# Attention scores in whole chunks with wider masks, pairs of heads in straight code, projections in four pieces

## The reference

```
scores = jnp.einsum('bhqd,bhkd->bhqk', qh, k_rec) / math.sqrt(d)
t = jnp.arange(s, dtype=jnp.float32)
decay = jnp.exp(-LAMBDA_DECAY * jnp.abs(t[:, None] - t[None, :]))
scores = scores * decay[None, None, :, :]
attn = jax.nn.softmax(scores, axis=-1)
out = jnp.einsum('bhqk,bhkd->bhqd', attn, v_rec)
```

## Time and profile before

| | |
|---|---|
| median of three runs | 1450.16 us (1449.71 to 1453.62) |
| the profiled execution | 1457.08 us, span 1453.1 us |
| busy in the span: TensorE, ScalarE, VectorE, GpSimd | 1307.9, 1059.6, 711.9, 624.5 us |
| mean granted TensorE clock | 0.956 |
| score matmuls, product matmuls | 2432, 4096 |
| exponentials of a half | 1024, busy 866.0 us |
| masks, far reads | 512 and 248 |

### The profile page before, as it was taken

How to read it: one execution, slowest core, us unless ns; L and a number is a source line. 1 busy time by engine, 2 the same in 40 slices (tenths; PEclk the granted TensorE clock), 3 DMA queues, 4 the chain that set the end, 5 groups by cost and what they waited for, 6 DMA issues and landing times. The chain is left out here.

```text
span 1453.1 us, 27412 instructions
## 1 busy us (share of the span) xinstructions
PE 1307.9 (90%) x8496; PEld 582.6 (40%) x8497; DVE 711.9 (49%) x1948; ACT 1059.6 (73%) x1419; POOL 624.5 (43%) x745
## 2 busy tenths in 40 slices
PE   7879999999999999999999999999987867889881
PEld 4623333333333333333333333333335546657541
DVE  5525535454453535445354443333324566685754
ACT  4558898987989888898988899999953534544532
POOL 2525444443445444444444444444202543333574
PEclk9979999999999999999999999999988987999996
DMA  7775566654566655556665566546962224457843
GB/s 195 252 179 132 136 153 159 128 146 109 134 152 147 158 119 145 124 124 160 143 161 103 145 126 134 105 97 135 244 127 73 91 91 153 160 189 225 248 126 106
DMA packets 141170, 212.00 MB, mean 146 GB/s; under 512 B 56864, under 2 KB 102816, under 8 KB 132768
## 3 DMA queue, kind: packets, MB, share of 16 engines
q1 hardware_dynamic: 134496, 192.86, 53.6%
q0 software_dynamic: 6144, 16.79, 3.6%
q10 hardware_dynamic: 384, 0.52, 0.1%
HBM read 147.19 MB, written 67.11 MB: 147 GB/s over the span
## 5 line engine op out<-in xcount | busy, mean ns | idle before, releaser
L841 ACT ACTIVATE work<-ps 128x1024 f32<-128x1024 f32 (+1 forms) x1024 | 866.0, 928 | 139.4 <-DVE ps L638 109.2
L764 PE MATMUL ps<-work 128*32 128x512 f32 x4096 | 551.4, 611 | 4.3 <-POOL work L607 3.6
L752 PE MATMUL ps<-Q_st,K_st 64*128 64x512 f32 (+3 forms) x2432 | 422.8, 423 | 33.6 <-ACT work L841 14.3
L604 POOL TENSOR_TENSOR work<-work 128x512 f32<-128x512 f32 x248 | 257.9, 1040 | 413.5 <-DVE work L646 413.5
L752 PEld LDWEIGHTS ps<-Q_st,K_st 64*128 64x128 f32 x2432 | 225.0, 185 | 515.8 <-ACT work L841 259.9
L646 DVE TENSOR_SCALAR work<-ps 128x512 f32<-128x512 f32 x248 | 171.2, 690 | 286.5 <-PE ps L752 286.1
L638 DVE TENSOR_TENSOR ps<-ps,small 128x128 f32<-128x128 f32 x512 | 150.6, 298 | 261.7 <-PE ps L752 254.9
L607 POOL TENSOR_SCALAR work<-work 128x512 f32<-128x512 f32 x248 | 154.3, 622 | 49.1 <-POOL work L604 49.1
L764 PEld LDWEIGHTS ps<-work 128*32 128x32 f32 x4096 | 82.1, 108 | 128.5 <-issue 73.5
L2219 POOL DMA_INDIRECT xT<-y_dram,decay x64 | 65.5, 1023 | 62.8 <-DMA xT<-y_dram,decay 27.7
L2201 POOL DMA_INDIRECT xs_dram<-part,decay x64 | 66.5, 1039 | 56.2 <-DMA xs_dram<-part,decay 24.7
(11 more groups left out here) (184 smaller groups left out, 1149.9 us busy)
## 6 DMA issues: line engine op xcount, KB each, us to landing
K_st<-halves_dram SPq DMA_DIRECT2D x248, 256.0 KB, 5.5
halves_dram<-work SPq DMA_DIRECT2D x64, 512.0 KB, 3.9
Q_st<-halves_dram SPq DMA_DIRECT2D x248, 128.0 KB, 5.8
work<-xs_dram SPq DMA_DIRECT2D x96, 128.0 KB, 2.6
y_dram<-work SPq DMA_DIRECT2D x48, 256.0 KB, 2.8
work<-in_L_attn_x SPq DMA_DIRECT2D x16, 512.0 KB, 7.3
attn_dram<-work SPq DMA_DIRECT2D x16, 256.0 KB, 6.9
work<-attn_dram SPq DMA_DIRECT2D x8, 512.0 KB, 4.5
```

The costliest lines, as they stand in the source:

```text
L604: nc.gpsimd.tensor_tensor(p, p, p, ALU.mult).then_inc(s_["far_sq"], 1)
L752: m = nc.tensor.matmul(ps[:, half_of(turn, s, k) + c % 2, q0 % CH:q0 % CH + w], K_st[tile, par, a, kt * P:(kt + 1) * P], Q_st[tile, par, a ...
L764: m = nc.tensor.matmul(ps[STRIP * c:STRIP * (c + 1), ACC + par], Vg[:, par, kt], probs[:, probs_of(turn, s), chunk(c)], start=s == 0, stop ...
L841: nc.scalar.activation(probs[:, probs_of(turn, s), chunks[0] * CH:(chunks[-1] + 1) * CH], src, ACT.Exp, scale=SCALE).then_inc(s_["exp_done ...
```

## The change

- A chunk of scores is always one matmul. `decay_of` chooses the factors for the whole chunk: for the own chunk FALL if the tile lies in its first half, RISE if in its second. `score_pieces` and `cut` go.
- With it the mask has to mend all that lies on the wrong side of the own block within the chunk: 128, 256, 256 or 128 columns for the four places of a tile in its chunk (`own_chunk`). It reads a window of one table of 512 columns, `wide_mask`, which is loaded in the prologue by one DMA of 256 KB instead of two of 64 KB.
- The own half is the second one in every tile (`OWN = 1`).
- On TensorE the order of a step is now: scores of both halves, then the products of step s-2.
- A projection's two products are issued separately: at steps 6 and 7 for the first, 11 and 12 for the second, behind the products of the step. VectorE's three pieces for the second move from steps 12, 13, 14 to 13, 14, 15.
- All 16 pairs are written out, without a loop.
- GpSimd no longer increments a semaphore of its own between the square and what follows.

```diff
 def pairs(eng, pair):
-    pair(0, True, True, False, 0)
-    with eng.Fori(1, 1 + 3 * RING, RING) as it:
-        for j in range(RING):
-            pair(it + j, True, False, False, (1 + j) % RING)
-    for it in range(1 + 3 * RING, NPAIR - 1):
-        pair(it, it < NPAIR - PPU, False, False, it % RING)
-    pair(NPAIR - 1, False, False, True, (NPAIR - 1) % RING)
+    for it in range(NPAIR):
+        pair(it, it < NPAIR - PPU, it == 0, it == NPAIR - 1, it % RING)
...
+    def decay_of(kt, c):
+        if c == kt // CT:
+            return FALL if kt % CT < CT // 2 else RISE
+        return FALL if c > kt // CT else RISE
...
+    OWN = 1
     def half_at(kt, k):
-        return k if first_half(kt) == 0 else 1 - k
+        own = kt * P // HALF
+        return own if k == OWN else 1 - own
...
+    def own_chunk(turn, s, kt):
+        bank, at = half_of(turn, s, OWN) + kt // CT % 2, kt % CT
+        if at < CT // 2:
+            width = (at + 1) * P
+            return ps[:, bank, 0:width], wide[:, CH // 2 - width:CH // 2]
+        return ps[:, bank, at * P:CH], wide[:, CH // 2:CH // 2 + (CT - at) * P]
...
 (GpSimd, far_probs)
-                pool.sem_inc(far_link, 1)
...
 (VectorE)
-                wait(dve, "sc_ps", n * NHALF + 2 * s + own_at(kt) + 1)
-                nc.vector.tensor_tensor(own_block(turn, s, kt), own_block(turn, s, kt), dmask, ALU.mult).then_inc(s_["masked"], 1)
+                wait(dve, "sc_ps", n * NHALF + 2 * s + OWN + 1)
+                own, mended = own_chunk(turn, s, kt)
+                nc.vector.tensor_tensor(own, own, mended, ALU.mult).then_inc(s_["masked"], 1)
...
-                        if prep and par == 0 and s >= 12 and s < 15:
-                            prepare(s - 12, it % PPU, 1, 2 * it + 1, idle)
+                        if prep and par == 0 and s >= 13:
+                            prepare(s - 13, it % PPU, 1, 2 * it + 1, idle)
...
 (TensorE)
-                for q0, w, a in score_pieces(kt, half):
-                    c = q0 // CH
+                for c in (2 * half, 2 * half + 1):
+                    a = decay_of(kt, c)
                     tile = slice(c % 2 * TILE_ROWS, (c % 2 + 1) * TILE_ROWS)
...
+                    m = nc.tensor.matmul(ps[:, half_of(turn, s, k) + c % 2], K_st[tile, par, a, kt * P:(kt + 1) * P],
+                                         Q_st[tile, par, a, half * CH:(half + 1) * CH], start=True, stop=True)
...
-                        scores(first, turn, n, s, 0, order, not end)
+                        for k in range(2):
+                            scores(first, turn, n, s, k, order, not end)
                         if s >= 2:
                             products(turn, n, s - 2, order, not end)
...
-                        scores(first, turn, n, s, 1, order, not end)
...
-                            if s == 7:
+                            if s == 6:
                                 wait(pe, "w", it + 1)
                                 if not first:
                                     wait(pe, "att_sb", n)
-                                project(at, 0, idle)
+                                project(at, 0, 0, idle)
+                            if s == 7:
+                                project(at, 0, 1, idle)
                             if s == 11:
                                 wait(pe, "proj_free", 2 * it + 1)
-                                project(at, 1, idle)
+                                project(at, 1, 0, idle)
+                            if s == 12:
+                                project(at, 1, 1, idle)
```

More of the change, by code:

```diff
@@ L237, in _ @@
                     sp.dma_start(decay[STRIP * r:STRIP * (r + 1), sign, :], io["c_decay"][sign]).then_inc(dec_in, 16)
-            for mask, dst in enumerate(diagonal_masks(small)):
-                sp.dma_start(dst, io["c_diag"][mask]).then_inc(dec_in, 16)
+            sp.dma_start(wide_mask(small), io["c_wide"]).then_inc(dec_in, 16)
             for n in range(4, NB):
@@ L439, in attention @@
     part = carve(work, 13312, 2, 2, 2, CH)
-    dmask, _ = diagonal_masks(small)
+    wide = wide_mask(small)
     rden = carve(small, 256, CT, QC)
@@ L722, in _, with project @@
             prime(pe, *"proj_ps sc_ps pv_done oT_ps".split())
-            def project(at, which, bank):
-                for k in range(KD):
-                    m = nc.tensor.matmul(ps[:, bank], w_unit[:, which, k], xT[:, k, at:at + CH] if isinstance(at, int) else xT[:, k, bass.ds(at, CH)],
-                                         start=k == 0, stop=k == KD - 1)
-                m.then_inc(s_["proj_ps"], 1)
+            def project(at, which, k, bank):
+                m = nc.tensor.matmul(ps[:, bank], w_unit[:, which, k], xT[:, k, at:at + CH], start=k == 0, stop=k == KD - 1, skip_group_check=True)
+                if k == KD - 1:
+                    m.then_inc(s_["proj_ps"], 1)
             def far_read(first, n, s, k, order):
@@ L747, in scores @@
                     far_read(first, n, s, k, order)
-                for q0, w, a in score_pieces(kt, half):
-                    c = q0 // CH
+                for c in (2 * half, 2 * half + 1):
+                    a = decay_of(kt, c)
                     tile = slice(c % 2 * TILE_ROWS, (c % 2 + 1) * TILE_ROWS)
-                    at = c // 2 * CH + q0 % CH
-                    m = nc.tensor.matmul(ps[:, half_of(turn, s, k) + c % 2, q0 % CH:q0 % CH + w],
-                                         K_st[tile, par, a, kt * P:(kt + 1) * P], Q_st[tile, par, a, at:at + w], start=True, stop=True)
+                    m = nc.tensor.matmul(ps[:, half_of(turn, s, k) + c % 2], K_st[tile, par, a, kt * P:(kt + 1) * P],
+                                         Q_st[tile, par, a, half * CH:(half + 1) * CH], start=True, stop=True)
                 m.then_inc(s_["sc_ps"], 1)
@@ L2554, in constants @@
     diag = np.where(s > q, np.exp(-2 * DECAY * (s - q)), 1.0)
+    before, after = np.arange(-P, P)[None, :], np.arange(2 * P)[None, :]
+    wide = np.concatenate([np.where(s > before, np.exp(-2 * DECAY * (s - before)), 1.0),
+                           np.where(after > s, np.exp(-2 * DECAY * (after - s)), 1.0)], axis=1)
     pack = lambda v: np.ascontiguousarray(v, dtype=np.float32).view(np.uint32)[:, ::2] >> 16 | np.ascontiguousarray(v, dtype=np.float32).view(np.uint32)[:, 1::2]
@@ L2559, in constants @@
     route = np.concatenate([pack(above).view(np.float32), pack(np.ones((P, P))).view(np.float32), np.tile(line, (P, 1)).astype(np.float32)], axis=1)
-    out = {"c_ident": np.eye(P), "c_decay": decay, "c_diag": np.stack([diag, diag.T]), "c_route": route, "c_zero": np.zeros((P, D))}
+    out = {"c_ident": np.eye(P), "c_decay": decay, "c_diag": np.stack([diag, diag.T]), "c_wide": wide, "c_route": route, "c_zero": np.zeros((P, D))}
     return {k: np.ascontiguousarray(v, dtype=np.float32) for k, v in out.items()}
```

18 lines of the change are left out of this document (6 added, 12 removed).

## The result

The changed kernel takes 1397.78 us (median of four, 1396.08 to 1399.0) against 1450.09 for the kernel before on the same chip (1449.71 to 1453.62): a ratio of 0.9633 [0.9615, 0.9651], 52.3 us less. The forecast was 1405, the range 1394 to 1428. The profiled execution took 1399.0, its span 1397.2 instead of 1453.1.

What follows compares the result with a forecast made beforehand. TensorE was taken to bound the kernel, with scores stalled by a ring of mask and exps, plus loop jumps. Plain heads 19.0, jumps 8.9, projecting heads 15.4, register waits 2.0: 1450.2 - 45.3 = 1405 us, range 1394 to 1428.

Steps and rivals of the forecast that it cites:

- Unrolling: Writing out the looped pairs 1 to 9 removes 8.9 us of jumps and 2.0 of register waits.
- two jumps: Two jumps back at the ends of loop turns, 4.46 us each, 8.9 removed.
- register waits: Waits on registers in nine looped heads with projections, 0.22 us each, 2.0 removed.
- rival 4: Straight code is not free: each of nine pairs pays the jump's 4.46 us, 40 us, 1445; chance 0.03.
- The plain head: A head without projections goes from 28.40 to 27.4 us; 19 of them save 19.0.
- the ring: Far read, mask, exps, then the score waiting for them, across two pairs of tiles; costs 0.3 us per plain head.
- rivals 1 and 2: Ring binds, 0.25 us late: 1423, chance 0.18; second score's wait holds value products, 0.5 late: gain gone, chance 0.05.
- The projecting head: A head with projections goes from 33.4 to 32.0 us (27.4 + 4.24 + 0.4); eleven save 15.4.
- rival 3: Split products cost 0.2 us more at each of 48 visits, or preparations stall 1.43: 1416; chance 0.14.
- the same work: Projection products on TensorE cost alike per head: two paired visits 4.26 us before, four single visits 4.24 after.
- The stall of 0.4: VectorE's second projection preparation ends 0.55 us late; 0.4 reaches TensorE, in steps 0 and 1 of the next head.
- The sum: Plain heads 19.0, jumps 8.9, projecting heads 15.4, register waits 2.0: together 45.3 us off 1450.2.

Runs made afterwards that it cites:

- unroll_only: The kernel before with all pairs in straight code and nothing else changed; 1438.59 us, 0.9898 of the kernel before.
- mask512: The changed kernel with every mask 512 columns wide (scores not the reference's); 1439.82 us, 0.9899 of the kernel before.
- after_third: The changed kernel run and profiled once more, unchanged; 1398.66 us, 0.9611 of the kernel before.
- unsplit: The changed kernel with each projection's two products together, behind steps 7 and 11, and VectorE's second preparation back at steps 12 to 14; 1393.26 us.
- mask_first: The changed kernel with VectorE's mask ahead of its far read in far tiles; 1407.68 us, 0.969 of the kernel before.
- unsplit_spread: The kernel unsplit with VectorE's second preparation spread over steps 12, 14 and 15; 1392.69 us, 0.9577 of the kernel before.
- unsplit_late: The kernel unsplit with VectorE's second preparation at steps 12 and 14 and its subtraction at step 0 of the next head; 1394.85 us.

## Why the prediction was right

- **Unrolling.** 8.9 for two jumps, 2.0 for register waits: 10.9 forecast, 10.5 in unroll_only (8.9 and 1.6). That the 1.6 are register waits isn't shown. Straight code was costed at nothing and costs nothing (rival 4): weight loads never stand 2.90 for issue in after, and plain heads of unroll_only stay at 28.40.
- **The plain head.** 27.4 forecast, 27.33 measured: 19 x 1.07 = 20.3 instead of 19.0. The terms held: scores to P 0.66, P to scores 1.00, far read 0.53 behind its score, read to mask 0.61, wide mask 0.43. mask512 shows that the ring sits right above: 0.33 more mask costs 1.06 a head, what rivals 1 and 2 had said of it. So they were priced rightly there and lay beyond a mask's length that wasn't reached.
- **The projecting head.** 32.0 forecast, 31.96 (32.17 in after_third): 15.4 forecast, and 907.4 - 871.7 - 20.3 = 15.4 measured. The visit at 1.05 instead of 1.06 falls on the row's side of rival 3: loading and draining make 0.2, not the 0.4 that I had worked out from the rule on a mode change in the Trainium skill (TensorEngine Tiling (Array Packing), "Key Properties"). But unsplit shows what the sum hid. Moving the products behind P makes a visit cheaper (1.91 a pair instead of 2.13), and splitting them gives it back; "the same work" was two changes that cancel.
- **The stall of 0.4** in that head was right in size (31.96 - 27.33 - 4.20 = 0.43) and in place, between P of steps 0 and 1 of the next head. Its cause was right for the larger part: VectorE's pieces make a mask late, ScalarE waits for it and a score for ScalarE, 0.27. The other 0.17, or 0.42 in the dearer heads, is P's wait for GpSimd, which shuts out VectorE's subtraction and is shut out by it. The prediction has no such term; that 0.27 and 0.17 together make the 0.4 is luck. In the thirty heads of before none of the 22 subtractions meets a GpSimd operation, and all take 1.21; the change moved eleven of them onto a square. The first head of before had such a meeting and its price (2.08, above). The Trainium skill has the rule (SBUF — State Buffer, "Who interferes with whom"): VectorE and GpSimd share a port pair as an exclusive lock, and a VectorE operation with two inputs in SBUF contends with a GpSimd operation that reads SBUF. The traces agree: what is left of a square and then 1.21 would be 2.2, and 2.09 is measured; masks, with one input in PSUM, leave the square at 1.04. The same section of the Trainium skill says that the order of issue decides who waits. Where one starts 0.16 or more ahead, the traces agree (subtraction first by 0.16 in mask_first: 1.21 and 1.95; square first by 0.43 in mask512: 1.04 and 1.69). Where the square's record starts 0.03 ahead, the square is nevertheless the one that waits in 3 of 11 heads of after and in 11 of 11 of unsplit_spread; what decides there is open.
- **The sum.** 45.3 forecast, 46.2 in the thirty heads (917.9 to 871.7). The median fell by 52.3 and the span by 55.9; the rest lies outside the heads, which I had taken at nothing, up to 1 us either way each for the first and the last. Both profiles of before have 533 to 535 there; the twelve others, all in straight code, 522.5 to 530.0, about 526 on the average, and unroll_only already 527.0. Whether straight code gives 7 us there or two profiles of before are high by chance isn't settled: the spread among kernels that differ in nothing there is as large. Part of it goes with the granted TensorE clock behind the last transposes: that stretch takes 363.9 and 362.1 at a mean of 0.88 in before's two profiles and 357.6 and 358.2 at 0.90 in unroll_only and after, but also 360.9 and 362.3 at 0.88 in after_third and unsplit_late, which are straight.

## What to carry to other kernels

Price a ring by its arms (read, mask, exponential, score) before it binds, and know how far it is from binding: here 0.3 us more of mask would have taken back nearly all that the change gave a plain head. Put a visit to other shapes on TensorE behind an operation that changes shape anyway, and make it one visit: splitting cost 0.38 of visits a head, and the kernel without it is 0.27 a head faster. Before a VectorE operation with both inputs in SBUF is moved, look at what GpSimd does at the new place.

## What the runs showed of the hardware

- VectorE's subtraction of two inputs in SBUF and GpSimd's square shut each other out, and when their records start within 0.04 us, who yields varies from head to head at the same step: the subtraction takes 2.09 with the square at 1.04 (8 of 11 heads in after, 2 of 11 in after_third), or 1.22 with the square at 2.15 (3 and 9). The second way costs 0.22 us more per head here. With a lead of 0.16 or more the first one keeps its own length (1.21 beside 1.95 in mask_first, 1.04 beside 1.69 in mask512).
- A single product between two scores costs 0.19 more than the same product between P and a score (2.90 against 2.71, P to P).
